# The second layer normalisation moves from ScalarE to VectorE in a gated recurrent layer with a feed-forward part

## The chip, the cores and the metric

One core of one Trainium2 chip runs the kernel. The metric is the device time of one execution, in microseconds. It is compared with the same kernel before the change.

## The reference

The input x has 2 sequences of 4096 steps with 256 features. The layer computes, in float32:

```
u = x @ W_in + b_in;   g = sigmoid(x @ W_gate + b_gate)
h_t = tanh(h_(t-1) @ A + u_t @ Bm)              # 64 states, one step after the other
y_t = g_t * (h_t @ C.T + u_t @ D.T) + (1 - g_t) * x_t
x1  = norm(x + (y @ W_out + b_out + x))
f   = gelu(x1 @ bw1.T + b1) @ bw2.T + b2        # 1024 hidden units, weights are signs times a row scale
out = norm(x1 + f)
norm(v) = (v - mean(v)) / sqrt(var(v) + 1e-5)   # over the 256 features
```

The change touches only how the last line, the second norm, is carried out.

## The kernel before, in words

The 8192 rows are cut into 128 chunks, one for each partition, of 64 steps. Four steps make a block, so a block is 512 rows (four tiles t of 128 rows x 256 features), and there are NB = 16 blocks, numbered n. The first third of the time goes to the recurrence (two sweeps, and the gates). The second part runs all the rest in one software pipeline: `for n in range(-1, NB + 1)` each engine has its own function `iteration(n)`, in which pieces of several blocks stand in an order written out by hand. No planner is at work: the order in each function is the order on that engine's queue, and semaphores tie the queues together.

TensorE's iteration n makes the hidden products `hidden(n, c)` for eight chunks c (L886) and the products back to 256 features `ffn_out(n, c)` (L898), and between them the output product of the recurrence of block n+1 and n+2 (`out_products`, L862), transposes of x1 of block n+1 (L871), and `y_products` (L846) for n+2 and n+3. A hidden product goes through one of three PSUM banks: ScalarE takes the gelu (`hidden_gelu`, L527) and a float16 high part (`hidden_hi`, L535), VectorE makes the float16 low part (`hidden_lo`, L1188). `hidden(n, c)` may overwrite a bank only after the `hidden_lo` that last read it; `hidden(n + 1, 0)` so waits for `hidden_lo(n, 6)`. `ffn_out(n, c)` waits for `hidden_lo(n, c)`.

VectorE's iteration n runs, in this order: hidden_lo(n-1, 6); the second moments of block n-2 (`second_moments`, L1214); hidden_lo(n-1, 7); first sum and spread of block n+1; gate_y(n+2, 1) (L1140); hidden_lo(n, 0); the scale and residual sum of block n-1 (`ffn_scale` L1194, `second_sum` L1201); more of the first norm of block n+1, with hidden_lo(n, 1) to (n, 3) between; first_norm (L1172) and `second_spread(n-1, 0)` (L1206); then hidden_lo(n, 4), x1_lo(n+1, 0) (L1180), hidden_lo(n, 5), x1_lo(n+1, 1), gate_y(n+3, 0), second_spread(n-1, 1), and in iterations 0 to 2 one `keep_x` (L1067). x1_lo waits for ScalarE's x1_hi (L515).

GpSimd's iteration n: mix(n+2, 0) (L361, after gate_y), residual(n) (L377), second_rstd(n-2), mix(n+2, 1), hu_low (L353), ys_low(n+2, 0) (L365), the two first_rstd of block n+1 (L383, L385, after VectorE's first moments), hu_low, ys_low(n+2, 1), add_bias(n+2) (L371).

The second norm of block b: VectorE leaves mean and variance of each row in `moments[:, 1, t]`. GpSimd's second_rstd(b) adds eps (L390), takes minus the mean (L391), raises to the power -1/2 (L394) and multiplies the two (L396): a scale and a shift, kept for each block. ScalarE then applies them in place to `rows_of(gT, b)`, one activation of 128x256 for each tile (`second_norm`, L541): tile 0 in iteration b+2, tiles 1 to 3 in iteration b+3. SP stores the block (L301). For the last block ScalarE does tiles 0 and 1 (L608) and VectorE tiles 2 and 3 (L1316), and SP stores tiles 2 and 3 first (L310), then 0 and 1 (L312).

SP's own loop issues `load_x(n+2)`, which waits for first_sum of block n+1, and then `store(n-3)`.

Of the kernel before, what the change touches and what calls it, by code (L numbers as in the profile page):

```python
# [50 lines left out]
def gated_rnn_ffn(nc, x, W_in, b_in, W_gate, b_gate, A, Bm, C, D, W_out, b_out, w1, b1, w2, b2, out):  # L51
# [7 lines left out]
    NB = L // STEPS  # L59
# [13 lines left out]
    with ExitStack() as ctx:  # L73
        def sb(name, shape, dt=F32):
            return ctx.enter_context(nc.sbuf_tensor(name, shape, dt))

        def sem(name):
            return ctx.enter_context(nc.semaphore(name))
# [32 lines left out]
        neg_one = sb("neg_one", [P, STEPS])  # L111
# [19 lines left out]
        rstd2 = sb("rstd2", [P, NB, STEPS])  # L131
        shift2 = sb("shift2", [P, NB, STEPS])
# [65 lines left out]
        s_e2 = sem("second_norm_steps")  # L198
        s_rs2 = sem("second_scale_and_shift_ready")
# [65 lines left out]
        def due(b, first=0, end=NB):  # L265

            return first <= b < end
# [5 lines left out]
        def _(sp):  # L273
# [29 lines left out]
            for n in range(-1, NB + 2):  # L303
                if due(n + 2, 1):
                    load_x(n + 2)
                if due(n - 3, 0, NB - 1):
                    store(n - 3)
            at = L - STEPS
            sp.wait_ge(s_or_last, 1)
            sp.dma_start(out_rows[:, at + 2:at + 4, :], rows_of(gT, NB - 1)[:, 2:4, :]).then_inc(s_st, 16)  # L310
            sp.wait_ge(s_or, NB)
            sp.dma_start(out_rows[:, at:at + 2, :], rows_of(gT, NB - 1)[:, 0:2, :]).then_inc(s_st, 16)  # L312
# [4 lines left out]
        def _(pool):  # L317
# [4 lines left out]
            pool.memset(neg_one[:, :], -1.0)  # L322
# [64 lines left out]
            def second_rstd(b, tiles, moments_done, steps_done):  # L387

                pool.wait_ge(s_v2, moments_done)
                pool.tensor_tensor(rstd2[:, b, tiles], moments[:, 1, tiles, 1], eps[:, tiles], ALU.add)  # L390
                pool.tensor_tensor(shift2[:, b, tiles], moments[:, 1, tiles, 0], neg_one[:, tiles],  # L391
                                   ALU.mult).then_inc(s_e2, 1)
                pool.wait_ge(s_e2, steps_done + 1)
                pool.tensor_tensor(rstd2[:, b, tiles], rstd2[:, b, tiles], neg_half[:, tiles], ALU.pow).then_inc(s_e2, 1)  # L394
                pool.wait_ge(s_e2, steps_done + 2)
                pool.tensor_tensor(shift2[:, b, tiles], shift2[:, b, tiles], rstd2[:, b, tiles],  # L396
                                   ALU.mult).then_inc(s_rs2, 1)
# [3 lines left out]
            def iteration(n):  # L401
# [4 lines left out]
                if due(n - 2, 0, NB - 1):  # L406
                    second_rstd(n - 2, ALL_TILES, n - 1, n * 2 - 4)
# [37 lines left out]
            second_rstd(NB - 1, slice(0, 2), NB, NB * 2 - 2)  # L445
            second_rstd(NB - 1, slice(2, 4), NB + 1, NB * 2)
# [3 lines left out]
        def _(act):  # L450
# [87 lines left out]
            def second_norm(b, t):  # L538

                act.wait_ge(s_rs2, b + 1)  # L540
                done = nc.scalar.activation(rows_of(gT, b)[:, t, :], rows_of(gT, b)[:, t, :], ACT.Identity,  # L541
                                            bias=shift2[:, b, t:t + 1], scale=rstd2[:, b, t:t + 1])
                if t == STEPS - 1:
                    done.then_inc(s_or, 1)

            def iteration(n):
# [5 lines left out]
                if due(n - 3, 0, NB - 1):  # L552
                    second_norm(n - 3, 1)
# [9 lines left out]
                if due(n - 3, 0, NB - 1):  # L563
                    second_norm(n - 3, 2)
# [8 lines left out]
                if due(n - 3, 0, NB - 1):  # L573
                    second_norm(n - 3, 3)
                if due(n - 2, 0, NB - 1):
                    second_norm(n - 2, 0)
# [29 lines left out]
            act.wait_ge(s_rs2, NB)  # L606
            for t in range(2):
                done = nc.scalar.activation(rows_of(gT, NB - 1)[:, t, :], rows_of(gT, NB - 1)[:, t, :], ACT.Identity,  # L608
                                            bias=shift2[:, NB - 1, t:t + 1], scale=rstd2[:, NB - 1, t:t + 1])
            done.then_inc(s_or, 1)  # L610

# [350 lines left out]
        def _(dve):  # L962
# [246 lines left out]
            def second_moments(n):  # L1209
                dve.wait_ge(s_sp2, n * 2 + 2)  # L1210
                if n > 0:
                    dve.wait_ge(s_rs2, n)
                for t in range(STEPS):
                    done = nc.vector.bn_aggr(moments[:, 1, t, :], stats[:, 1, t, :])  # L1214
                done.then_inc(s_v2, 1)

            def iteration(n):
# [89 lines left out]
            dve.wait_ge(s_rs2, NB - 1)  # L1307
# [5 lines left out]
            dve.wait_ge(s_rs2, NB + 1)  # L1313
            for t in PAIRS[1]:
                row = rows_of(gT, NB - 1)[:, t, :]
                done = nc.vector.tensor_scalar(row, row, rstd2[:, NB - 1, t:t + 1], shift2[:, NB - 1, t:t + 1],  # L1316
                                               ALU.mult, ALU.add)
            done.then_inc(s_or_last, 1)
# [24 lines left out]
```

## Time and profile before

| | us |
|---|---|
| median of 3 runs | 513.57 (511.14 to 516.47) |
| profiled execution, its own time | 514.47 |
| span of its trace | 512.6 |
| busy: PE | 475.2 (93%) |
| busy: VectorE | 374.2 (73%) |
| busy: ScalarE | 302.7 (59%) |
| busy: GpSimd | 278.2 (54%) |

The profile names engines PE (matmul), PEld (weight load), DVE (VectorE), ACT (ScalarE), POOL (GpSimd) and SP (the queue that issues the loads and stores). L886 is line 886 of the kernel before. Times are from the first instruction. A duration reaches from the issue of an instruction to its end; instructions of one engine overlap by some hundredths of a microsecond, so the distance from one start to the next is what each adds to a queue. "[0.39 <-ACT hid L535]" says that the engine sat idle for 0.39 us before this row and what released it. The granted clock is that of TensorE, 1.00 for its full speed.

### The profile page before, as it was taken

To read this page: it belongs to the slowest core of one execution; us is meant where nothing else is said; L and a number is where in the kernel's file an instruction comes from. 1 tells how busy PE (TensorE), PEld (TensorE's weight loads), DVE (VectorE), ACT (ScalarE), POOL (GpSimd) and SP (SyncE) were. 2 spreads that over 40 slices of the span, in tenths; PEclk is the share of its full clock that TensorE was granted. 3 is DMA by queue.
4 is the path that set the end of the run, shared out by engine and by line. 5 is a ranking of instruction groups with operands and counts; after the bars stand their busy time and mean duration, and the time that the engine had idled before them with its cause. 6 is when DMAs were issued, how large, how long until landed. Compare 5 with 4: busy or idle time off the path is not lost.

```text
span 512.6 us, 8565 instructions
## 1 busy us (share of the span) xinstructions
PE 475.2 (93%) x2847; PEld 321.1 (63%) x2847; DVE 374.2 (73%) x784; ACT 302.7 (59%) x550; POOL 278.2 (54%) x289
## 2 busy tenths in 40 slices
PE   9999999999998469989899999999999999999891
PEld 6666566556554247666667766776767767776651
DVE  1455555796976428789898798798797897887664
ACT  1122222443443418748688788797797797787683
POOL 4100010152516748697697787877967976963403
PEclk9999999999999859999999999999999999999997
DMA  7333451000010101101022022021021120220113
GB/s 210 117 107 98 123 196 51 2 0 0 0 43 0 41 1 42 42 1 42 1 83 82 2 83 82 3 83 52 32 83 32 53 83 6 79 83 1 42 41 123
DMA packets 9268, 28.76 MB, mean 56 GB/s; under 512 B 1776, under 2 KB 2544, under 8 KB 9104
## 3 DMA queue, kind: packets, MB, share of 16 engines
q1 hardware_dynamic: 7904, 27.27, 15.7%
q0 software_dynamic: 272, 0.66, 0.4%
q10 hardware_dynamic: 1056, 0.36, 0.3%
q8 instruction: 21, 0.34, 0.3%
q14 instruction: 15, 0.12, 0.1%
HBM read 19.90 MB, written 8.39 MB: 55 GB/s over the span
## 4 chain that ended last, share of the span: by engine, by line
PE 72%; DVE 14%; issue 5%; POOL 5%; ACT 4%; DVEq 0%; POOLq 0%; ACTq 0%
PE bank L886 17%; PE bank L898 16%; PE bank L627 8%; PE bank L724 7%; PE bank L634 7%; DVE hid L1188 5%; PE bank L862 4%; PE bank L846 4%; PE bank L619 4%; DVE gT L1201 3%; ACT hid L535 2%; PE bank L871 2%; DVE bank L1194 2%; DVE bank L1151 2%; PE bank L710 1%
## 5 line engine op out<-in xcount | busy, mean ns | idle before, releaser
L886 PE MATMUL bank<-xT,w1s 128*128 128x512 f16 x512 | 132.3, 382 | 10.0 <-DVE hid L1188 9.7
L898 PE MATMUL bank<-w2s,hid 128*128 128x256 f16 x1024 | 127.6, 273 | 1.3 <-DVE gT L1201 0.8
L1188 DVE SCALAR_TENSOR_TENSOR hid<-bank,small,hid 128x512 f16<-128x512 f32 x128 | 94.1, 737 | 46.8 <-ACT hid L535 46.8
L898 PEld LDWEIGHTS bank<-w2s,hid 128*128 128x128 f16 x1024 | 98.8, 98 | 34.2 <-issue 4.8
L527 ACT ACTIVATE bank<-bank,b_col,alpha 128x512 f32<-128x512 f32 x128 | 95.3, 746 | 36.2 <-PE bank L886 36.0
L535 ACT ACTIVATE hid<-bank,small 128x512 f16<-128x512 f32 x128 | 85.6, 683 | 32.6 <-PE bank L898 31.5
L348 POOL TENSOR_TENSOR xg_lo<-xT,xg_hi 128x512 fp32r<-128x512 f32 x12 | 22.9, 1925 | 104.9 <-DVE xg_hi L991 104.9
L886 PEld LDWEIGHTS bank<-xT,w1s 128*128 128x128 f16 x512 | 45.5, 98 | 54.1 <-issue 12.1
L365 POOL TENSOR_TENSOR ys_lo<-gT,ys_hi 128x512 fp32r<-128x512 f32 x32 | 41.5, 1300 | 45.0 <-ACT ys_hi L511 43.9
L361 POOL TENSOR_TENSOR gT<-gT,xT 128x512 f32<-128x512 f32 x32 | 41.7, 1307 | 16.3 <-DVE gT L1140 14.6
L478 ACT ACTIVATE hu<-bank 64x128 f32 (+1 forms) x64 | 17.4, 272 | 53.6 <-PE bank L634 53.6
L634 PE MATMUL bank<-hu,w_rec 128*64 (+1 forms) x208 | 45.2, 299 | 0.8 <-DVE hu L1013 0.8
L627 PE MATMUL bank<-xT,w_in 128*128 (+1 forms) x128 | 44.9, 435 | 0.0
L371 POOL TENSOR_TENSOR x_load<-x_load,half_b_out 128x1024 f32<-128x1024 f32 x16 | 38.2, 2390 | 10.8 <-DMA x_load<-in_L_attn_x 10.8
L862 PE MATMUL bank<-w_out_hi,ys_hi 128*128 128x256 f32 x128 | 40.7, 318 | 1.4 <-POOL ys_lo L365 1.4
L377 POOL TENSOR_TENSOR gT<-x_rows,b_row 128x1024 f32<-128x1024 f32 x16 | 40.0, 2498 | 2.1 <-DVE x_rows L1172 2.1
L634 PEld LDWEIGHTS bank<-hu,w_rec 128*64 128x64 f32 x208 | 20.0, 135 | 28.7 <-issue 25.7
L466 ACT ACTIVATE hu<-bank 64x128 f32 x40 | 10.9, 271 | 45.7 <-PE bank L634 45.7
L965 DVE COPY xT<-bank 128x256 f32 (+1 forms) x64 | 26.4, 423 | 15.5 <-PE bank L619 14.3
L970 DVE TENSOR_SCALAR hu<-bank,b_in_col 64x256 f32 (+1 forms) x32 | 15.7, 491 | 29.3 <-PE bank L627 29.3
L353 POOL TENSOR_TENSOR hu_lo<-hu,hu_hi 64x512 fp32r<-64x512 f32 x28 | 35.4, 1265 | 2.2
L862 PE MATMUL bank<-w_out_lo,ys_hi 128*128 128x256 f32 x128 | 36.6, 286 | 0.0
(128 smaller groups left out, 843.6 us busy)
## 6 DMA issues: line engine op xcount, KB each, us to landing
x_load<-in_L_attn_x SPq DMA_DIRECT2D x16, 512.0 KB, 3.4
gT<-in_L_attn_x SPq DMA_DIRECT2D x15, 512.0 KB, 3.4
out_rows<-gT SPq DMA_DIRECT2D x15, 512.0 KB, 2.6
gT<-in_L_ffn_w SPq DMA_DIRECT2D x2, 1024.0 KB, 7.2
gT<-in_L_attn_x SPq DMA_DIRECT2D x4, 128.0 KB, 3.0
out_rows<-gT SPq DMA_DIRECT2D x2, 256.0 KB, 2.2
w_gate<-in_L_attn_W_gate ACTq DMA_DIRECT2D x1, 256.0 KB, 7.6
x_rows<-in_L_attn_W_out POOLq DMA_DIRECT2D x1, 256.0 KB, 6.5
```

What stands on the lines that cost most here:

```text
L361: pool.tensor_tensor(gT[:, b, m, :], gT[:, b, m, :], xT[:, b, m, :], ALU.subtract).then_inc(s_ys, 1)
L365: pool.tensor_tensor(ys_lo[:, m, :], gT[:, b, m, :], ys_hi[:, m, :].bitcast(F32), ALU.subtract).then_inc(s_ylo, 1)
L371: pool.tensor_tensor(x_load[:, :, :], x_load[:, :, :], half_b_out[:, None, :].broadcast_to([P, STEPS, DM]), ALU.add).then_inc(s_xb, 1)
L377: pool.tensor_tensor(rows_of(gT, b), x1_rows[:, :, :], b2_row[:, None, :].broadcast_to([P, STEPS, DM]), ALU.add).then_inc(s_x1b, 1)
L527: nc.scalar.activation(bank[which][:, :], bank[which][:, :], ACT.Gelu, bias=b1_col[:, c:c + 1], scale=alpha1[:, c:c + 1]).then_inc(s_gelu, 1)
L535: nc.scalar.activation(hid[:, c % 3, 0, :], bank[HIDDEN_BANKS[c % 3]][:, :], ACT.Copy, scale=hid_scale[:, 0:1]).then_inc(s_hhi, 1)
L627: done = nc.tensor.matmul(bank[4 + half][:, 0:N // 2], w_in[:, k, :], xT[:, j, k, half * (N // 2):(half + 1) * (N // 2)], start=(k == 0), ...
L634: nc.tensor.matmul(bank[6 + parity][0:NS, 0:P], w_rec[:, :], hu[:, t, :], start=True, stop=True).then_inc(done_sem, 1)
L862: done = nc.tensor.matmul(bank[6 + pair][:, e * DM:(e + 1) * DM], ys, w[:, k, :], start=(i == 0), stop=(i == len(parts) - 1))
L886: done = nc.tensor.matmul(bank[which][:, :], w1s[:, k, c * P:(c + 1) * P], x1T[:, n, part, :, k, :], start=(k == 0 and part == 0), stop=(k ...
L898: done = nc.tensor.matmul(bank[tile // 2][:, tile % 2 * DM:(tile % 2 + 1) * DM], hid[:, c % 3, part, tile * P:(tile + 1) * P], w2s[:, c, : ...
L1188: nc.vector.scalar_tensor_tensor(out=hid[:, c % 3, 1, :], in0=bank[HIDDEN_BANKS[c % 3]][:, :], scalar=hid_scale[:, 0:1], in1=hid[:, c % 3, ...
```

## The change

The second norm of every block is carried out by VectorE, in place, as (v - mean) times the inverse root, both read as scalars for each partition. In iteration n it stands in two pairs of tiles: one after hidden_lo(n, 4), one after hidden_lo(n, 5), both for block n-2. GpSimd keeps only the sum with eps and the power; the shift, its constant and the arrays for each block go. ScalarE has no part in it any more. SP stores block n-2 in iteration n, and for the last block tiles 0 and 1 before 2 and 3. In iteration NB, where no hidden chunks are left, the two pairs of block NB-2 stand behind hidden_lo(NB-1, 7) and ahead of the last ffn_scale.

```diff
-        neg_one = sb("neg_one", [P, STEPS])
...
-        rstd2 = sb("rstd2", [P, NB, STEPS])
-        shift2 = sb("shift2", [P, NB, STEPS])
+        rstd2 = sb("rstd2", [P, STEPS])
...
@@ SP
-                if due(n - 3, 0, NB - 1):
-                    store(n - 3)
+                if due(n - 2, 0, NB - 1):
+                    store(n - 2)
             at = L - STEPS
+            sp.wait_ge(s_or, NB)
+            sp.dma_start(out_rows[:, at:at + 2, :], rows_of(gT, NB - 1)[:, 0:2, :]).then_inc(s_st, 16)
             sp.wait_ge(s_or_last, 1)
             sp.dma_start(out_rows[:, at + 2:at + 4, :], rows_of(gT, NB - 1)[:, 2:4, :]).then_inc(s_st, 16)
-            sp.wait_ge(s_or, NB)
-            sp.dma_start(out_rows[:, at:at + 2, :], rows_of(gT, NB - 1)[:, 0:2, :]).then_inc(s_st, 16)
@@ GpSimd
-            pool.memset(neg_one[:, :], -1.0)
...
-            def second_rstd(b, tiles, moments_done, steps_done):
-
-                pool.wait_ge(s_v2, moments_done)
-                pool.tensor_tensor(rstd2[:, b, tiles], moments[:, 1, tiles, 1], eps[:, tiles], ALU.add)
-                pool.tensor_tensor(shift2[:, b, tiles], moments[:, 1, tiles, 0], neg_one[:, tiles],
-                                   ALU.mult).then_inc(s_e2, 1)
-                pool.wait_ge(s_e2, steps_done + 1)
-                pool.tensor_tensor(rstd2[:, b, tiles], rstd2[:, b, tiles], neg_half[:, tiles], ALU.pow).then_inc(s_e2, 1)
-                pool.wait_ge(s_e2, steps_done + 2)
-                pool.tensor_tensor(shift2[:, b, tiles], shift2[:, b, tiles], rstd2[:, b, tiles],
-                                   ALU.mult).then_inc(s_rs2, 1)
+            def second_rstd(b, tiles, done):
+
+                pool.wait_ge(s_v2, done)
+                pool.tensor_tensor(rstd2[:, tiles], moments[:, 1, tiles, 1], eps[:, tiles], ALU.add).then_inc(s_e2, 1)
+                pool.wait_ge(s_e2, done)
+                pool.tensor_tensor(rstd2[:, tiles], rstd2[:, tiles], neg_half[:, tiles], ALU.pow).then_inc(s_rs2, 1)
...
@@ ScalarE (second_norm and its calls in iteration, and the two tiles of the last block)
-            def second_norm(b, t):
-
-                act.wait_ge(s_rs2, b + 1)
-                done = nc.scalar.activation(rows_of(gT, b)[:, t, :], rows_of(gT, b)[:, t, :], ACT.Identity,
-                                            bias=shift2[:, b, t:t + 1], scale=rstd2[:, b, t:t + 1])
...
@@ VectorE
             def second_moments(n):
                 dve.wait_ge(s_sp2, n * 2 + 2)
-                if n > 0:
-                    dve.wait_ge(s_rs2, n)
...
+            def second_norm(b, pair, done):
+
+                dve.wait_ge(s_rs2, done)
+                for t in PAIRS[pair]:
+                    row = rows_of(gT, b)[:, t, :]
+                    last = nc.vector.tensor_scalar(row, row, moments[:, 1, t, 0:1], rstd2[:, t:t + 1],
+                                                   ALU.subtract, ALU.mult)
+                return last
...
                 if due(n):
                     hidden_lo(n, 4)
+                if due(n - 2, 0, NB - 1):
+                    second_norm(n - 2, 0, n - 1)
                 if due(n + 1, 1):
                     x1_lo(n + 1, 0)
                 if due(n):
                     hidden_lo(n, 5)
+                if due(n - 2, 0, NB - 1):
+                    second_norm(n - 2, 1, n - 1).then_inc(s_or, 1)
                 if due(n + 1, 1):
                     x1_lo(n + 1, 1)
...
-            dve.wait_ge(s_rs2, NB - 1)
             for pair in range(2):
                 dve.wait_ge(s_sp2, NB * 2 - 1 + pair)
                 for t in PAIRS[pair]:
                     done = nc.vector.bn_aggr(moments[:, 1, t, :], stats[:, 1, t, :])
                 done.then_inc(s_v2, 1)
-            dve.wait_ge(s_rs2, NB + 1)
-            for t in PAIRS[1]:
-                row = rows_of(gT, NB - 1)[:, t, :]
-                done = nc.vector.tensor_scalar(row, row, rstd2[:, NB - 1, t:t + 1], shift2[:, NB - 1, t:t + 1],
-                                               ALU.mult, ALU.add)
-            done.then_inc(s_or_last, 1)
+            second_norm(NB - 1, 0, NB).then_inc(s_or, 1)
+            second_norm(NB - 1, 1, NB + 1).then_inc(s_or_last, 1)
```

## Rows read from the trace of the kernel before

**Rows 1.** The page: the chain that ended last, its shares of the span by engine.
```profile
PE 72%; DVE 14%; issue 5%; POOL 5%; ACT 4%; DVEq 0%; POOLq 0%; ACTq 0%
```

**Rows 2.** Busy time in one block: stretch, its length, engines, clock, DMA share, GB/s.
```profile
366.08:385.85 19.77, 19.39 (x135) 14.03 (x136) 16.64 (x41) 15.88 (x27) 15.49 (x17) 1.00 0.15 54
```

**Rows 3.** Timeline of VectorE, end of block 8: start us, us, instruction, count.
```profile
360.49 0.74 DVE L1188 SCALAR_TENSOR_TENSOR hid<-bank,small,hid 128x512 f16<-128x512 f32 x1
361.55 0.69 DVE L1180 SCALAR_TENSOR_TENSOR xT<-bank,xT 128x512 f16<-128x512 f32 x1 [0.32 <-ACT xT L515]
362.16 0.74 DVE L1188 SCALAR_TENSOR_TENSOR hid<-bank,small,hid 128x512 f16<-128x512 f32 x1
362.85 0.69 DVE L1180 SCALAR_TENSOR_TENSOR xT<-bank,xT 128x512 f16<-128x512 f32 x1
...
364.06 0.74 DVE L1206 BATCH_NORM_STATS2 stats<-gT 128x6 f32<-128x256 f32 x2
365.18 0.75 DVE L1188 SCALAR_TENSOR_TENSOR hid<-bank,small,hid 128x512 f16<-128x512 f32 x1 [0.39 <-ACT hid L535]
```

**Rows 4.** Timeline of TensorE in block 8: hidden(8, 4) and its wait.
```profile
355.93 1.04 PE L886 MATMUL bank<-xT,w1s 128*128 128x512 f16 x4 [0.36 <-DVE hid L1188]
```

**Rows 5.** Timeline around the end of block 14: hidden_lo(14, 6) and hidden(15, 0).
```profile
482.27 0.75 DVE L1188 SCALAR_TENSOR_TENSOR hid<-bank,small,hid 128x512 f16<-128x512 f32 x1 [0.57 <-ACT hid L535]
...
483.17 1.02 PE L886 MATMUL bank<-xT,w1s 128*128 128x512 f16 x4 [1.75 <-DVE hid L1188]
```

**Rows 6.** Groups by line and shape: busy us, mean ns of one | idle before.
```profile
L541 ACT ACTIVATE gT<-gT,shift,rstd 128x256 f32<-128x256 f32 x60 | 33.9, 595 | 0.9 <-POOL shift L396 0.9
L1172 DVE TENSOR_SCALAR x_rows<-bank,moments,rstd 128x256 f32<-128x256 f32 x64 | 31.3, 531 | 0.2 <-POOL rstd L385 0.2
...
L1316 DVE TENSOR_SCALAR gT<-gT,rstd,shift 128x256 f32<-128x256 f32 x2 | 0.7, 410 | 2.7 <-POOL shift L396 2.7
...
L1081 DVE TENSOR_SCALAR half_b_out<-half_b_out 128x256 f32<-128x256 f32 x1 | 0.3, 284 | 0.0
```

**Rows 7.** Timeline of the end of the kernel, from the last blocks' norms on.
```profile
500.70 1.01 POOL L394 TENSOR_TENSOR rstd<-rstd,neg_half 128x4 f32<-128x4 f32 x1
...
501.96 1.30 DVE L1194 TENSOR_TENSOR bank<-bank,alpha_row 128x512 f32<-128x512 f32 x2 [1.14 <-PE bank L898]
...
508.77 0.73 DVE L1316 TENSOR_SCALAR gT<-gT,rstd,shift 128x256 f32<-128x256 f32 x2 [2.73 <-POOL shift L396]
...
509.91 0.43 SPq L312 DMA_DIRECT2D out_rows<-gT  x1
```

**Rows 8.** Timeline of VectorE and GpSimd in the first part, around 105 us.
```profile
103.43 2.28 DVE L1034 SCALAR_TENSOR_TENSOR gT<-gT 128x2048 f16<-128x2048 f32 x1
103.59 6.53 POOL L348 TENSOR_TENSOR xg_lo<-xT,xg_hi 128x512 fp32r<-128x512 f32 x2 [7.66 <-DVE xg_hi L991]
...
105.63 3.37 DVE L1036 SCALAR_TENSOR_TENSOR gT<-gT 128x2048 f16<-128x2048 f32 x1
```

**Rows 9.** The copies of L1277: count, ns min/median/max, first and last start, forms.
```profile
L1277 DVE COPY hu<-hu x8: 208/219/1194, 151.5 to 158.4; 64x128 f32<-64x128 f32 x8
```

**Rows 10.** Timeline of GpSimd, end of block 8, beside rows 3.
```profile
359.96 1.27 POOL L365 TENSOR_TENSOR ys_lo<-gT,ys_hi 128x512 fp32r<-128x512 f32 x1
361.19 2.37 POOL L371 TENSOR_TENSOR x_load<-x_load,half_b_out 128x1024 f32<-128x1024 f32 x1
```

**Rows 11.** Timeline of GpSimd and VectorE in blocks 13 and 14.
```profile
459.35 0.74 DVE L1188 SCALAR_TENSOR_TENSOR hid<-bank,small,hid 128x512 f16<-128x512 f32 x1
...
461.14 2.37 POOL L377 TENSOR_TENSOR gT<-x_rows,b_row 128x1024 f32<-128x1024 f32 x1
...
478.00 0.74 DVE L1188 SCALAR_TENSOR_TENSOR hid<-bank,small,hid 128x512 f16<-128x512 f32 x1
478.15 2.36 POOL L377 TENSOR_TENSOR gT<-x_rows,b_row 128x1024 f32<-128x1024 f32 x1 [2.13 <-DVE x_rows L1172]
```

**Rows 12.** Busy time and clock in the long idle before the first hidden product.
```profile
176.00:184.00 8.00, 0.32 (x1) 0.35 (x2) 0.00 (x0) 0.96 (x2) 7.27 (x6) 0.50 0.00 0
```

More of the change, by code:

```diff
@@ L197, in gated_rnn_ffn @@
         s_v2 = sem("second_moments_ready")
-        s_e2 = sem("second_norm_steps")
-        s_rs2 = sem("second_scale_and_shift_ready")
+        s_e2 = sem("second_variance_with_eps")
+        s_rs2 = sem("second_rstd_ready")
         s_x1 = sem("x1_ready")
@@ L406, in iteration @@
                 if due(n - 2, 0, NB - 1):
-                    second_rstd(n - 2, ALL_TILES, n - 1, n * 2 - 4)
+                    second_rstd(n - 2, ALL_TILES, n - 1)
                 if due(n + 2, 2):
@@ L444, in _ @@
                 iteration(n)
-            second_rstd(NB - 1, slice(0, 2), NB, NB * 2 - 2)
-            second_rstd(NB - 1, slice(2, 4), NB + 1, NB * 2)
+            second_rstd(NB - 1, slice(0, 2), NB)
+            second_rstd(NB - 1, slice(2, 4), NB + 1)
         @block.scalar
@@ L536, in hidden_hi @@
                                      scale=hid_scale[:, 0:1]).then_inc(s_hhi, 1)
-            def second_norm(b, t):
-                act.wait_ge(s_rs2, b + 1)
-                done = nc.scalar.activation(rows_of(gT, b)[:, t, :], rows_of(gT, b)[:, t, :], ACT.Identity,
-                                            bias=shift2[:, b, t:t + 1], scale=rstd2[:, b, t:t + 1])
-                if t == STEPS - 1:
-                    done.then_inc(s_or, 1)
             def iteration(n):
@@ L551, in iteration @@
                     hidden_hi(n - 1, 7)
-                if due(n - 3, 0, NB - 1):
-                    second_norm(n - 3, 1)
                 if due(n):
@@ L562, in iteration @@
                     hidden_gelu(n, 2)
-                if due(n - 3, 0, NB - 1):
-                    second_norm(n - 3, 2)
                 if due(n + 3, 2):
@@ L572, in iteration @@
                     hidden_hi(n, 3)
[L573 to L576, printed above, removed]
                 if due(n):
@@ L605, in _ @@
                 iteration(n)
[L606 to L610, printed above, removed]
         @block.tensor
```

## The prediction, made before the change was timed

> **What bounds the kernel now.** Read the page first: the chain that ended last runs on PE for 72% and on DVE for 14% [rows 1], so TensorE carries the time and VectorE cuts in. Then one block of the second half, from hidden(n, 0) to hidden(n+1, 0). I number blocks by n; block 9 is 366.08 to 385.85, and the ten blocks 3 to 12 repeat it every 19.77 us. In that time ACT is busy 15.88, POOL 15.49, DVE 16.64, PE 19.39 [rows 2]. The averages do not say what ends a block; the queues do. hidden(n+1, 0) needs hidden_lo(n, 6) from VectorE. In block 8 that instruction starts at 365.18 [rows 3], and the matmul that opens block 9 at 366.08, 0.90 later. Block 14 shows that 0.90 is the hand-over itself: hidden_lo at 482.27, matmul at 483.17, and there PE had waited 1.75 us for it [rows 5]. So in blocks 3 to 12 PE and VectorE arrive together, and VectorE has no slack towards TensorE.
>
> What slack VectorE has inside its stream is in two places, both inside the stretch where the change inserts work [rows 3]. After hidden_lo(4) at 360.49 the next instruction could start 0.69 later (as 362.16 to 362.85), at 361.18, but x1_lo waits to 361.55: 0.37. The last pair of statistics starts at 364.06; its two take 0.74 and the next could start some 0.67 later, at 364.73, but hidden_lo(6) waits for ScalarE to 365.18: 0.45. Together 0.82 us a block.
>
> **The change part by part.** *ScalarE* loses 60 activations of 595 ns in the blocks [rows 6], 2.4 us each block, and two at the end. I cost this at nothing gained. Both waits of VectorE for ScalarE above are for work that TensorE had released just before (x1_hi follows the transposes, hidden_hi(6) follows hidden_gelu(7)), and no second_norm stands between; the other PE wait, 0.36 before hidden(n, 4) [rows 4], is for hidden_lo(1), which stands in VectorE's own queue behind the scale and sum instructions. ys_high comes earlier by 0.6, but GpSimd's next result for VectorE follows VectorE's own moments.
>
> *GpSimd* loses the multiply by -1 and the shift product, about 0.3 us of queue with the dependent wait, in a stretch after which it idles for ys_high. Nothing. The constant memset at the start is hidden under the input loads.
>
> *SP* stores a block one iteration earlier. The store waits for the second pair's norm and stands ahead of the next load_x, which waits for a first_sum half a block later. Nothing queues.
>
> *VectorE* gains four tensor_scalar of 128x256 a block. The form is there: two at the end, 410 ns each, 0.73 for the two [rows 6, 7], so they start 0.32 apart and a pair adds 0.66 to the stream. Four add 1.32. Against 0.82 of slack that alone is 0.50 a block.
>
> *The collision.* I do not stop there. The same operation reading PSUM takes 531, from SBUF 410, which is 121 less; one with constants in SBUF takes 284 [rows 6]. 128 of 256 columns at one a cycle would be about that difference: the SBUF form seems to take two elements at a time. The Trainium skill ("VectorE: DVE Perf Modes", the perf-mode tier table) says that fp32 tensor_scalar within SBUF runs at 2x, using both read ports; the 410 beside 531 agrees. By its cycle estimate one norm would be about 290 ns, by the row it is 410; the sum takes the row.
>
> This matters since instructions of VectorE that read SBUF twice at a time and GpSimd's shut each other out in this trace [rows 8]. VectorE's L1034 runs 2.28 us from 103.43; GpSimd's two L348, from 103.59, take 6.53 together, where one of 512 elements takes 1.27 [rows 10]. VectorE's next, L1036, is issued at 105.63 and takes 3.37 against its twin's 2.28, 1.09 more: it let the L348 that was waiting pass first, nearly whole. They alternate, each waiting for one full instruction of the other. L1034 has two sources in SBUF; that one source is enough is seen in the eight small SBUF copies of L1277, 219 ns in the median and 1194 at most [rows 9], the long ones beside GpSimd's work. The Trainium skill ("SBUF — State Buffer", SBUF: two separate sides) calls it an exclusive lock held for the full instruction; these rows agree.
>
> Now place the first pair. It is issued at 361.18. GpSimd ends ys_low(1) at 361.23 and starts add_bias (L371, 2.37 us) at 361.19 [rows 10]. Both engines are tied to VectorE's moments there, so this meeting recurs in each block. The first norm gets in, ends at about 361.56, add_bias follows from about 361.43 to 363.80, and the second norm, issued at 361.50, comes behind it and ends 0.29 later, at 364.09. (If add_bias wins the first turn both norms come after it, with the same end.) The pair takes 2.91 instead of 0.73, so 2.18 more. The second pair falls after add_bias; GpSimd's next instruction, mix, waits for a gate_y that stands behind it on VectorE, so it is free.
>
> Blocks 3 to 12: 1.32 + 2.18 - 0.82 = 2.68, times 10 = 26.8. Block 2 also carries keep_x and has no second slack: 3.50 - 0.37 = 3.1. Block 13: GpSimd has add_bias and residual back to back, the second from 461.14 for 2.37 [rows 11]; hidden_lo(4) starts at 459.35 [rows 11], so the pair is issued at 460.04; its first norm passes between the two, the second after residual, and it ends near 463.98, 3.94 instead of 0.73. That is 3.21 + 1.32, less the slack of this block, 0.37 + 0.65 (the idle before hidden_lo(6) is 0.57, as in block 14 [rows 5]): 3.5. Block 14: hidden_lo(4) at 478.00, residual 478.15 to 480.51 [rows 11]; the pair, issued at 478.69, ends at 481.12, 2.43 instead of 0.73: 1.70 + 1.32 - 1.02 = 2.0. Block 15: VectorE idles more than a pair before each place: 0. Sum 35.4.
>
> *The end.* norm(14) now stands on VectorE ahead of the last ffn_scale (501.96). It waits for the pow that starts at 500.70 [rows 7], 0.15 earlier without the multiply, so it runs from 501.6 to 502.9: +0.95. At the very end four small GpSimd instructions go from the path (0.87 with their waits), of which I give back 0.4 since norm and the second pow meet: -0.5. The store that SP issues last is no longer second in line (it began at 509.91, and the norm before it ended at 509.50): -0.38. Together +0.1.
>
> **Sum.** 35.5 us on the profiled execution's 514.47 gives 550.0. That execution lies 0.9 above the median of 513.57, so I forecast 549.
>
> The unknown cost is the wait of a norm behind GpSimd. Below it is nothing (0.50 a block); the longest blocking of VectorE that I show is 1.09 (3.37 - 2.28), by a 512-element instruction; above it is 2.37 a turn, full length of add_bias. I take 2.18, since rows 8 show full length each time and L371 is the instruction that stands there. With +-0.3 us on each block the forecast's own range is 544 to 554.
>
> **Rivals.**
> *No collision* (the two pointer scalars keep the norm to one port, or both norms slip in before add_bias). For it: 410 ns is also what one element a cycle could give, and the second norm misses its turn by only 0.3 us. Against: 121 ns less than from PSUM, and both queues keep step with the same moments. Time: 0.50 x 10 + 1.0 + 0.3 x 2 - 0.3 = +6.3, 520. Chance 0.10.
> *Short lock* (a GpSimd instruction of 1024 elements lets go half way, 1.09): 1.59 x 10 + 2 + 3 + 0 = +21, 534. Chance 0.07.
> *Not slower*: its place is the 0.82 us of slack a block. If norms follow each other by 0.20 instead of 0.32, as their place behind a wait might hide, and no lock bites, four fit into it; this decides at 0.205 a norm. Blocks 3 to 15 then cost 0, block 2 0.4, the end -0.3: 514. ScalarE's free 2.4 us speaks for it, the measured 0.32 against. Chance 0.03.
> *Slower still*: the longer wait of PE, 2.7 us in one piece, makes the clock fall. After the long idle of 176 to 184 it was granted 0.50 (1.2 of 2.4 GHz) [rows 12]; the wait of 1.75 in block 14 left the four matmuls behind it at 1.02 us, as in a block at full clock [rows 4, 5]. PE's part of the loop, hidden(0) to ffn_out(6), is five groups of eight or four matmuls, some 0.9 each (the four of hidden(0) show 1.02); these 4.4 us would double: 4.4 x 12 = 53 more, 602. Chance 0.03.
> The forecast has 0.77.
>
> **Numbers.** Less than 1% of 513.57, about 5 us, can't be told from no change. Slower by more: 0.77 + 0.07 + 0.03 and half of no collision, 0.92. Within: the other half and most of not slower, 0.06. Faster 0.02. The range takes in the forecast with its bounds (to 558, if both norms of a pair wait a turn in some blocks) and goes down to 527, which leaves out no collision and takes in the short lock: 0.77 x 0.95 + 0.07 = 0.80.
>
> **What would show it.** In the profile after: blocks of about 22.4 us; a pair of norms of 2.9 us on VectorE that begins right after hidden_lo(4), beside L371; the second pair 0.73; x1_lo(0) without a wait; PE waiting some 2.7 us before hidden(n+1, 0), released by hidden_lo(6); ScalarE down by 36 us. If both pairs are 0.73 and blocks last 20.3, the collision was wrong and the stream argument right; if blocks last 19.8, both were. A granted clock under 1.00 between 250 and 450 would be the last rival.

## The result: 9% slower, and the profile after

The changed kernel took 565.12 us in the median (557.43 to 567.45 in 4 runs) against 512.42 for the kernel before. The ratio is 1.0915, with a 95% interval of 1.0853 to 1.0977; it is below the quotient of the medians because it leaves out the two runs that took over 1.5% longer than the quickest. The profiled execution shown below is the one of 565.87 us. Its granted clock is 0.949, as in the run of 564.38 us; the quickest run, 557.43 us, has 0.960. The forecast was 549, with 558 as the upper end.

Its page, first the span, then busy time by engine, the slices of the granted clock, and the chain that ended last [rows 1]:

```profile
span 563.9 us, 8515 instructions
...
PE 497.8 (88%) x2847; PEld 330.1 (59%) x2847; DVE 419.6 (74%) x846; ACT 274.3 (49%) x488; POOL 275.3 (49%) x254
...
PEclk9999999999998799989898998989989898899997
...
PE 47%; DVE 40%; issue 5%; POOL 4%; ACT 2%; DVEq 0%; POOLq 0%; ACTq 0%
```

VectorE's share of the chain went from 14% to 40%: TensorE now waits for it in every block. ScalarE's busy time fell from 302.7 to 274.3 us, and the kernel was slower all the same (what that relief is worth by itself is experiment 8). And the clock slices are dented in the second half, where [rows 2] had 1.00 throughout a block.

The group of the new instruction, and how its single durations spread (count, ns min/median/max):

```profile
L1190 DVE TENSOR_SCALAR gT<-gT,moments,rstd 128x256 f32<-128x256 f32 x64 | 50.1, 824 | 2.0 <-POOL rstd L389 2.0
```

```profile
L1190 DVE TENSOR_SCALAR gT<-gT,moments,rstd x64: 397/403/2470, 241.6 to 561.1; 128x256 f32<-128x256 f32 x64
```

A mean of 824 over a median of 403 says that a few instances are very long. The timeline of VectorE at the end of block 8 shows which (it answers to [rows 3]; L1158 is hidden_lo, L1150 x1_lo, L1190 the norm):

```profile
385.54 0.74 DVE L1158 SCALAR_TENSOR_TENSOR hid<-bank,small,hid 128x512 f16<-128x512 f32 x1
386.19 2.78 DVE L1190 TENSOR_SCALAR gT<-gT,moments,rstd 128x256 f32<-128x256 f32 x2
388.89 0.68 DVE L1150 SCALAR_TENSOR_TENSOR xT<-bank,xT 128x512 f16<-128x512 f32 x1
389.50 0.73 DVE L1158 SCALAR_TENSOR_TENSOR hid<-bank,small,hid 128x512 f16<-128x512 f32 x1
390.15 0.72 DVE L1190 TENSOR_SCALAR gT<-gT,moments,rstd 128x256 f32<-128x256 f32 x2
...
392.66 0.73 DVE L1158 SCALAR_TENSOR_TENSOR hid<-bank,small,hid 128x512 f16<-128x512 f32 x1
```

and GpSimd at the same time (L362 is ys_low, L368 add_bias; compare [rows 10]):

```profile
385.00 1.27 POOL L362 TENSOR_TENSOR ys_lo<-gT,ys_hi 128x512 fp32r<-128x512 f32 x1
386.23 2.59 POOL L368 TENSOR_TENSOR x_load<-x_load,half_b_out 128x1024 f32<-128x1024 f32 x1
```

The first pair of norms takes 2.78 us and spans the whole of add_bias, which itself takes 2.59 instead of 2.37, since it starts beside the first norm. The second pair, with GpSimd idle, takes 0.72. Neither x1_lo nor hidden_lo(6), at 392.66, waits for ScalarE any more.

What TensorE does with that, at the start of block 9 (L856 is a hidden product, L816 y_products, L868 ffn_out), against [rows 4, 5]:

```profile
393.53 1.46 PE L856 MATMUL bank<-xT,w1s 128*128 128x512 f16 x4 [2.15 <-DVE hid L1158]
394.43 0.99 PE L816 MATMUL bank<-hu_hi,cd_hi 128*128 128x512 f32 x1
395.22 0.63 PE L816 MATMUL bank<-hu_hi,cd_lo 128*128 128x512 f32 x1
395.64 0.63 PE L816 MATMUL bank<-hu_lo,cd_hi 128*128 128x512 f32 x1
396.07 1.69 PE L868 MATMUL bank<-w2s,hid 128*128 128x256 f16 x8
397.60 1.03 PE L856 MATMUL bank<-xT,w1s 128*128 128x512 f16 x4
```

and by stretch, PE to POOL busy, then the granted clock; the first line is all of block 8 (block 9 in [rows 2] is its like), the next three follow the clock at the start of block 9, and the last two are the first 7 us of blocks 13 and 14:

```profile
369.72:393.53 23.81, 21.24 (x134) 14.79 (x135) 19.84 (x45) 14.08 (x22) 15.40 (x15) 0.93 0.13 45
393.00:394.00 1.00, 0.47 (x3) 0.26 (x4) 1.00 (x6) 0.00 (x0) 1.00 (x2) 0.99 0.02 4
394.00:397.00 3.00, 3.00 (x11) 1.76 (x10) 2.36 (x5) 1.38 (x2) 2.90 (x3) 0.50 0.00 0
397.00:398.00 1.00, 1.00 (x7) 0.65 (x6) 0.00 (x1) 0.00 (x0) 0.92 (x1) 0.81 0.00 0
...
489.04:496.04 7.00, 7.00 (x37) 4.63 (x38) 3.04 (x9) 1.68 (x3) 4.65 (x4) 0.76 0.01 2
512.91:519.91 7.00, 7.00 (x50) 5.21 (x51) 4.69 (x12) 3.96 (x6) 1.22 (x2) 1.00 0.02 6
```

TensorE waits 2.15 us for hidden_lo(6), begins at full clock, and is granted 0.50 (1.2 of 2.4 GHz) from about 394 to past 397, some 3.4 us. The eight ffn_out matmuls take 1.69 instead of the 1.05 that the same eight took in block 9 before. The four hidden matmuls from 397.60 take 1.03, as at full clock. The first 7 us of a block show 0.76 or 0.77 in all eleven blocks 3 to 13, and 1.00 in blocks 2 and 14.

**Where the 51.3 us are** (spans 563.9 and 512.6). Blocks 3 to 12 last 238.3 us together instead of 197.7, 4.06 more each. In block 9 this splits at 399.60, the start of hidden_hi(9, 0) on ScalarE: up to there it is 6.07 us from the block's start, before 4.44 (+1.63, all of it lost at the low clock); from hidden_lo(9, 0) to hidden_lo(9, 6) it is 16.14, before 13.71 (+2.43). The same stretch takes 6.07 or 6.08 in the other blocks up to 13, apart from 5.99 in block 3 and 6.34 in block 11 (which has 0.3 more in experiment 6 too, at full clock). With eleven blocks at the low clock: 11 x 1.63 = 17.9. The stream costs 10 x 2.43 = 24.3 in blocks 3 to 12, 2.86 in block 2 (no fall there), 4.52 - 1.63 = 2.9 in block 13 and 1.77 in block 14 (PE's wait ahead of it was 1.56, and no fall): 31.8. Block 15 with the end is +1.1 and what lies ahead of block 2 is +0.4. Sum 51.2. The +1.1 hides a twelfth fall of the clock: from hidden(15, 0) to hidden_hi(15, 0) it is 5.41 instead of 3.73, so 1.7 lost, against which the end itself is shorter (experiment 10).

### The profile page after: what moved, and what is told of

It is laid out like the page before. It is cut to its first block, busy times and chain, and to the rows that moved or that the text cites. A ratio compares the mean times of both kernels' runs of the same rounds, so it can differ in the third digit from the quotient of the medians.

```text
span 563.9 us, 8515 instructions
## 1 busy us (share of the span) xinstructions
PE 497.8 (88%) x2847; PEld 330.1 (59%) x2847; DVE 419.6 (74%) x846; ACT 274.3 (49%) x488; POOL 275.3 (49%) x254
## 4 chain that ended last, share of the span: by engine, by line
PE 47%; DVE 40%; issue 5%; POOL 4%; ACT 2%; DVEq 0%; POOLq 0%; ACTq 0%
DVE hid L1158 10%; PE bank L856 8%; DVE gT L1190 8%; PE bank L868 7%; PE bank L597 7%; PE bank L694 7%; PE bank L604 6%; DVE x_rows L1142 4%; DVE stats L1176 3%; PE bank L589 3%; PE bank L816 3%; DVE xT L1150 3%; DVE gT L1171 2%; ACT hid L527 2%; DVE bank L1164 2%
## 5 line engine op out<-in xcount | busy, mean ns | idle before, releaser
L856 PE MATMUL bank<-xT,w1s 128*128 128x512 f16 x512 | 138.6, 396 | 37.3 <-DVE hid L1158 37.2
L868 PE MATMUL bank<-w2s,hid 128*128 128x256 f16 x1024 | 134.1, 281 | 1.3 <-DVE gT L1171 0.8
L1158 DVE SCALAR_TENSOR_TENSOR hid<-bank,small,hid 128x512 f16<-128x512 f32 x128 | 93.9, 735 | 51.3 <-ACT hid L527 51.3
L868 PEld LDWEIGHTS bank<-w2s,hid 128*128 128x128 f16 x1024 | 102.2, 102 | 40.1 <-issue 8.5
L856 PEld LDWEIGHTS bank<-xT,w1s 128*128 128x128 f16 x512 | 46.2, 99 | 82.9 <-issue 41.3
L362 POOL TENSOR_TENSOR ys_lo<-gT,ys_hi 128x512 fp32r<-128x512 f32 x32 | 41.6, 1302 | 54.7 <-ACT ys_hi L503 53.7
L1190 DVE TENSOR_SCALAR gT<-gT,moments,rstd 128x256 f32<-128x256 f32 x64 | 50.1, 824 | 2.0 <-POOL rstd L389 2.0
L368 POOL TENSOR_TENSOR x_load<-x_load,half_b_out 128x1024 f32<-128x1024 f32 x16 | 40.7, 2543 | 10.8 <-DMA x_load<-in_L_attn_x 10.8
L350 POOL TENSOR_TENSOR hu_lo<-hu,hu_hi 64x512 fp32r<-64x512 f32 x28 | 35.5, 1267 | 2.2
```

The lines of the kernel that those rows point to most:

```text
L362: pool.tensor_tensor(ys_lo[:, m, :], gT[:, b, m, :], ys_hi[:, m, :].bitcast(F32), ALU.subtract).then_inc(s_ylo, 1)
L368: pool.tensor_tensor(x_load[:, :, :], x_load[:, :, :], half_b_out[:, None, :].broadcast_to([P, STEPS, DM]), ALU.add).then_inc(s_xb, 1)
L856: done = nc.tensor.matmul(bank[which][:, :], w1s[:, k, c * P:(c + 1) * P], x1T[:, n, part, :, k, :], start=(k == 0 and part == 0), stop=(k ...
L868: done = nc.tensor.matmul(bank[tile // 2][:, tile % 2 * DM:(tile % 2 + 1) * DM], hid[:, c % 3, part, tile * P:(tile + 1) * P], w2s[:, c, : ...
L1158: nc.vector.scalar_tensor_tensor(out=hid[:, c % 3, 1, :], in0=bank[HIDDEN_BANKS[c % 3]][:, :], scalar=hid_scale[:, 0:1], in1=hid[:, c % 3, ...
L1190: last = nc.vector.tensor_scalar(row, row, moments[:, 1, t, 0:1], rstd2[:, t:t + 1], ALU.subtract, ALU.mult)
```

## The experiments

Two theories stood after the result. The first: the growth of a block is a collision of the first pair with add_bias (about 2.05), plus the norms' own time beyond the slack (0.35), plus a clock loss that the longer wait of TensorE sets off (1.63). The second: the norms, their pointer scalars or their position cost this by themselves, and the clock merely goes with it. Each experiment takes one piece away. All are edits of the changed kernel, unless said otherwise. A block is the distance between hidden(n, 0) and hidden(n+1, 0) in blocks 3 to 12; it was 19.77 before and 23.81 after.

**1. add_bias cut to four columns** (the bias is then missing from most of x_load; the instruction stays in its place).

```diff
-pool.tensor_tensor(x_load[:, :, :], x_load[:, :, :], half_b_out[...].broadcast_to([P, STEPS, DM]), ALU.add)
+pool.tensor_tensor(x_load[:, 0, 0:4], x_load[:, 0, 0:4], half_b_out[:, 0:4], ALU.add)
```

> The changed kernel with GpSimd's add_bias cut from 1024 to 4 columns (most of half the output bias is left out of the sum; nothing else changes). Theory 1, the second norm of a pair waits behind add_bias: the first pair falls from 2.78 us to about 0.73, TensorE's wait before hidden(n+1, 0) from 2.15 to about 0.5, the granted clock stays at 1.00, a block lasts about 20.3 instead of 23.8, in all about 519 us. Theory 2, the norms are slow in the stream for a reason of their own (in place, two pointer scalars): the pair stays at 2.78 and the time near 557 to 565.

Measured: 521.41 us, ratio to the kernel before 1.0136 (1.0115 to 1.0156). VectorE and GpSimd at the meeting point, then TensorE behind it (the norm is L1189 here):

```profile
381.28 0.72 DVE L1189 TENSOR_SCALAR gT<-gT,moments,rstd 128x256 f32<-128x256 f32 x2
...
381.31 0.42 POOL L368 TENSOR_TENSOR x_load<-x_load,half_b_out 128x4 f32<-128x4 f32 x1
...
386.56 1.02 PE L855 MATMUL bank<-xT,w1s 128*128 128x512 f16 x4 [0.38 <-DVE hid L1157]
```

The pair is 0.72, TensorE waits 0.38 instead of 2.15, the block is 20.12 and the four matmuls take 1.02. One instruction on another engine, shortened, gives back 3.7 of 4.06 us a block. What is left, 0.35, is the four norms less the slack. Block 15, which follows a wait of 3.51 here, still began at a low clock (0.62 over its first 7 us).

**2. add_bias cut to 512 columns** (half of the bias is missing).

```diff
-pool.tensor_tensor(x_load[:, :, :], x_load[:, :, :], half_b_out[...].broadcast_to([P, STEPS, DM]), ALU.add)
+pool.tensor_tensor(x_load[:, 0:2, :], x_load[:, 0:2, :], half_b_out[...].broadcast_to([P, 2, DM]), ALU.add)
```

> The changed kernel with add_bias cut from 1024 to 512 columns (half of half the output bias is left out). Theory 1, a norm waits for the whole of add_bias: that instruction falls from 2.37 to about 1.3 us and the first pair from 2.78 to about 1.7; block 21.1, TensorE waits about 1.35 us and its clock holds; in all about 533 us. A lock held for a fixed time or let go half way: the pair at 2.0 or over.

Measured: 535.32 us, ratio 1.0393 (1.0324 to 1.0462). The same three places:

```profile
390.59 1.70 DVE L1190 TENSOR_SCALAR gT<-gT,moments,rstd 128x256 f32<-128x256 f32 x2
...
390.63 1.50 POOL L368 TENSOR_TENSOR x_load<-x_load,half_b_out 128x512 f32<-128x512 f32 x1
...
396.84 1.02 PE L856 MATMUL bank<-xT,w1s 128*128 128x512 f16 x4 [1.34 <-DVE hid L1158]
```

The pair's extra is 0.98 behind 512 columns and 2.06 behind 1024, so it follows the full length of GpSimd's instruction; the rival "short lock", by which the 1024 columns let go after 1.09, is out. The block is 21.09, and with a wait of 1.34 the clock held in blocks 4 to 13. It fell in block 3, behind 3.12, and in block 15, behind 3.52.

**3. A control: the kernel before, with add_bias cut to four columns in it.**

> Control: the kernel before with add_bias cut to 4 columns, as in the run of the changed kernel. Theory 1: add_bias is on no path of the kernel before, so 0 to 1 us less than before, and the gain of the cut in the changed kernel was the collision alone. Rival: shorter GpSimd work itself saves 10 us or more, here as there.

Measured: 511.66 us, ratio 0.9942 (0.9916 to 0.9968), blocks of 19.77 as before. Shortening add_bias gives about 3 us by itself, more than I expected, and none of it in blocks 1 to 15: block 0 begins at 185.81 instead of 187.66 and lasts 1.0 less, the latter by the clock, which was 0.85 over its first 7 us in the trace of the kernel before and 1.00 here. So the block times of experiments 1 and 2 are due to the meeting with the norms, but of the total of experiment 1 some 3 us are not. For the 512 columns of experiment 2 no such control was run.

**4. The norm's access pattern changed, everything else left** (252 instead of 256 columns of each tile, read as three runs of 84 that lie 85 apart, written as one run; the values written are then not all the right ones).

```diff
-nc.vector.tensor_scalar(row, row, moments[:, 1, t, 0:1], rstd2[:, t:t + 1], ...)
+nc.vector.tensor_scalar(row[:, 0:252].rearrange("p (a c) -> p a c", a=3),
+                        row[:, 0:255].rearrange("p (a c) -> p a c", a=3)[:, :, 0:84],
+                        moments[:, 1, t, 0:1], rstd2[:, t:t + 1], ...)
```

> The changed kernel with each second norm reading 3 rows of 84 columns (a pitch of 85) and writing 252 in one row, instead of 256 to 256: four columns are left out and the others shifted, the work is the same size, but the shape should keep VectorE from taking two elements at a time. Theory 1, a norm meets GpSimd only because it reads SBUF twice at a time: each norm alone takes longer (about 0.53 instead of 0.41), none waits for add_bias, the first pair takes about 1.0 instead of 2.78, a block lasts 20.6, in all about 526 us. Theory 2, any norm in SBUF waits for GpSimd: the pair stays at 2.8 or more, 557 to 565.

Measured: 526.64 us, ratio 1.0248 (1.0185 to 1.0311). The spread of the norm's durations, then the meeting:

```profile
L1190 DVE TENSOR_SCALAR gT<-gT,moments,rstd x64: 522/534/543, 241.7 to 521.5; 128x252 f32<-128x252 f32 x64
```

```profile
387.73 0.98 DVE L1190 TENSOR_SCALAR gT<-gT,moments,rstd 128x252 f32<-128x252 f32 x2
...
387.78 2.37 POOL L368 TENSOR_TENSOR x_load<-x_load,half_b_out 128x1024 f32<-128x1024 f32 x1
```

This is the cleanest answer. The norm is slower (534 for 252 columns against 403 for 256), yet the longest of 64 is 543 instead of 2470, add_bias takes its undisturbed 2.37, and the kernel takes 38 us less than the changed one in the median, 31 less than its quickest run. So the access pattern decides: as written, the norm is 131 ns quicker and is shut out; with the other pattern it is neither. That the quicker form takes two elements at a time fits the 131 ns, but the trace doesn't show it by itself. The Trainium skill ("VectorE: DVE Perf Modes", What auto-detection actually checks) lets an operation with one source run on two ports where source and destination are in SBUF and their outermost dimensions are both even or equal; three runs into one are neither, and the 534 agrees.

**5. Both pairs moved behind x1_lo(n+1, 1)**, the first by three VectorE instructions, the second by one, nothing left out.

```diff
-if due(n - 2, 0, NB - 1): second_norm(n - 2, 0, n - 1)
 ...
-if due(n - 2, 0, NB - 1): second_norm(n - 2, 1, n - 1).then_inc(s_or, 1)
 ...
+if due(n - 2, 0, NB - 1): second_norm(n - 2, 0, n - 1)
+if due(n - 2, 0, NB - 1): second_norm(n - 2, 1, n - 1).then_inc(s_or, 1)
```

> The changed kernel with both norm pairs moved two and one places later on VectorE, behind x1_lo(n+1, 1) and ahead of gate_y(n+3, 0), where add_bias is about to end and GpSimd's next instruction waits for that gate_y. Same instructions, same count. Theory 1, the meeting with add_bias costs: no norm takes much over its 0.41, four add 1.3 to 1.5 us against 0.45 of slack, a block lasts 20.7 to 20.8, the wait of TensorE is about 1 us and the clock holds; in all about 525 us. Theory 2, four more instructions on VectorE cost what they cost wherever they stand: 557 to 565.

Measured: 527.35 us, ratio 1.0244 (1.0218 to 1.0269).

```profile
389.24 0.69 DVE L1150 SCALAR_TENSOR_TENSOR xT<-bank,xT 128x512 f16<-128x512 f32 x1 [0.32 <-ACT xT L507]
...
391.15 1.38 DVE L1190 TENSOR_SCALAR gT<-gT,moments,rstd 128x256 f32<-128x256 f32 x4
...
394.58 1.02 PE L856 MATMUL bank<-xT,w1s 128*128 128x512 f16 x4 [0.84 <-DVE hid L1158]
```

The same work at another place in the same queue: the four norms take 1.38 together and the block 20.58. They cost 0.81 instead of the 0.35 of experiment 1, since the idle time before x1_lo(0), 0.32, is back and unused. The change as made cost 53 us in the median (45 in its quickest run), the same four norms a little further on cost 13: the rest was the place.

**6. The clock held up by other matmuls.** Nine matmuls of 512 columns into a bank that is free, right before hidden(n+1, 0); their result is overwritten.

```diff
+if due(n, 2, NB - 2):
+    pe.wait_ge(s_hlo, n * HC + 6)
+    for i in range(9):
+        nc.tensor.matmul(bank[HIDDEN_BANKS[2]][:, :], w1s[:, 0, 0:P], x1T[:, n, 0, :, 0, :], start=True, stop=True)
```

> The changed kernel with nine more matmuls of 512 columns on TensorE in blocks 2 to 13, into a free bank, between the output products and hidden(n+1, 0), so that TensorE works while it waits for VectorE. Theory 1, the wait of 2.15 us makes the clock fall to half for the 3 to 4 us behind it, and that costs 1.6 us a block: the clock stays at 1.00, hidden(n, 0) to hidden_hi(n, 0) takes 4.4 us again instead of 6.1, a block 22.2, in all about 545 us. Theory 2, TensorE's clock costs nothing since VectorE sets the pace: no change, or some us slower from the added matmuls.

Measured: 546.83 us, ratio 1.0630 (1.0608 to 1.0652). VectorE's pair (L1195 here), then TensorE with the added matmuls (L916), then five blocks of it by clock:

```profile
376.40 2.78 DVE L1195 TENSOR_SCALAR gT<-gT,moments,rstd 128x256 f32<-128x256 f32 x2
...
381.43 2.12 PE L916 MATMUL bank<-xT,w1s 128*128 128x512 f16 x9
383.74 1.02 PE L856 MATMUL bank<-xT,w1s 128*128 128x512 f16 x4 [0.19 <-DVE hid L1163]
```

```profile
282.80:394.00 111.20, 108.23 (x718) 74.17 (x716) 99.02 (x212) 70.40 (x111) 77.08 (x72) 1.00 0.15 49
```

The collision is untouched (2.78), TensorE does more work, and the kernel takes 18 us less than the changed one in the median, 11 less than its quickest run. Blocks last 22.18, which is 1.63 less than 23.81, and from hidden(n, 0) to hidden_hi(n, 0) it is 4.44 again instead of 6.07: this shows that the 1.63 was the clock's. It also comes near the forecast's sum with its clock assumption made true: +32 us on the 514.71 that the kernel before took beside it, where I had +35.5. Block 15 still began at a low clock, behind a wait of 3.53.

**7. Four such matmuls instead of nine.**

> As the run with nine added matmuls, but with four, so that TensorE still waits about 1.25 us before hidden(n+1, 0) instead of 0.2. If the clock is lost to the length of the wait, 1.25 us is as harmless as the 1.34 and 1.75 us seen before: clock 1.00, block 22.2, 547 us. If any wait in this place cools the clock, blocks of 23 to 24 us, 557 or more.

Measured: 548.73 us, ratio 1.0680 (1.0611 to 1.0749); blocks of 22.18 again.

```profile
382.54 1.04 PE L916 MATMUL bank<-xT,w1s 128*128 128x512 f16 x4
384.84 1.02 PE L856 MATMUL bank<-xT,w1s 128*128 128x512 f16 x4 [1.27 <-DVE hid L1163]
```

About 1 us of work, which cuts the wait to 1.27, is enough in blocks 4 to 13, all at 1.00. In block 3 the wait was still 3.04, and in block 15 it was 3.52; behind both the clock fell.

**8. The norm of blocks 0 to 14 left out on VectorE** (their output is then not normalised a second time); ScalarE and GpSimd are relieved as in the change.

> The changed kernel without the second norm of blocks 0 to 14 on VectorE (left out of the output; the store waits for the statistics instead), ScalarE and GpSimd as in the changed kernel. Theory 1, ScalarE's and GpSimd's relief is worth nothing and the whole loss comes from the norms on VectorE: blocks of 19.77 us, the end about 1.2 us shorter, 511 us. Rival, the relief of ScalarE is worth something that the norms hide: 505 us or less.

Measured: 512.97 us, ratio 0.9965 (0.9942 to 0.9988), blocks of 19.77. What is left of the change, the relief of ScalarE and GpSimd and the new end, is worth 1.8 us in all and nothing in the blocks up to 14; in the trace block 15 with the end is 28.00 instead of 29.45, which experiment 10 shows too. So no placement of the norms could have been much faster than the kernel before.

**9. A placement meant to be free**: tiles 0 and 1 behind gate_y(n+2, 1), half a block earlier, tile 2 alone behind hidden_lo(4), tile 3 alone behind x1_lo(1).

```diff
+second_norm(n - 2, (0, 1), n - 1)          # behind gate_y, before hidden_lo(n, 0)
 ...
+second_norm(n - 2, (2,), n - 1)            # behind hidden_lo(n, 4)
 ...
+second_norm(n - 2, (3,), n - 1).then_inc(s_or, 1)   # behind x1_lo(n + 1, 1)
```

> The changed kernel with the norms where VectorE idles and GpSimd does not stand in the way: tiles 0 and 1 behind gate_y(n+2, 1), where VectorE waits 2.4 us for hidden_hi(n, 0); tile 2 behind hidden_lo(n, 4) alone, so that it passes just ahead of add_bias (in blocks 14 and later with tile 3); tile 3 behind x1_lo(n+1, 1). The moments of block 14 move to the end of iteration 15, so that its norms run before the last scale. Theory 1: blocks 3 to 12 back at 19.77, block 2 and 13 some tenths longer, the end 1 us shorter than before: 512 us, level with the kernel before or 0.2% faster. If the place was not the matter, 520 or more.

Measured: 522.02 us, ratio 1.0156 (1.0133 to 1.0179); blocks of 20.65. This missed. VectorE, then GpSimd, around the early pair, and at last tile 2 with add_bias beside it:

```profile
355.70 2.70 DVE L1190 TENSOR_SCALAR gT<-gT,moments,rstd 128x256 f32<-128x256 f32 x2 [0.67 <-POOL rstd L389]
358.32 0.74 DVE L1158 SCALAR_TENSOR_TENSOR hid<-bank,small,hid 128x512 f16<-128x512 f32 x1
...
354.65 1.02 POOL L389 TENSOR_TENSOR rstd<-rstd,neg_half 128x4 f32<-128x4 f32 x1
355.64 1.26 POOL L358 TENSOR_TENSOR gT<-gT,xT 128x512 f32<-128x512 f32 x1
356.98 1.26 POOL L350 TENSOR_TENSOR hu_lo<-hu,hu_hi 64x512 fp32r<-64x512 f32 x1
...
367.99 0.41 DVE L1190 TENSOR_SCALAR gT<-gT,moments,rstd 128x256 f32<-128x256 f32 x1
...
368.01 2.61 POOL L368 TENSOR_TENSOR x_load<-x_load,half_b_out 128x1024 f32<-128x1024 f32 x1
```

The pair waits for GpSimd's root (L389), and the moment it is released is the moment GpSimd starts mix: each norm then sits out one GpSimd instruction, mix and hu_low, and takes 1.35 and 1.42, together 2.70. The two single norms did what was planned: tile 2 slips in ahead of add_bias in 0.41, tile 3 takes 0.47, and from hidden_lo(4) to hidden_lo(6) it is 4.70 us, before 4.69 [rows 3]. So the 0.88 by which a block grew is the early pair's, and a single norm at that place would most likely have waited too, as the first of the pair did.

**10. The kernel before with the new end alone** (block 15's four norms on VectorE, its two stores as in the change).

> The kernel before with only the end of the change: the last block's four tiles by VectorE with mean and root as scalars, no shift on GpSimd for it, tiles 0 and 1 stored first. The collision has no part in it. 0.9 us off GpSimd's chain and 0.3 off the last store: 1.2 us less than before, 0.2%; rival, the last store's own time hides it: no change.

Measured: 513.17 us, ratio 0.999 (0.9964 to 1.0015): no difference that can be told in the times. In its trace block 15 with the end is 28.03 instead of 29.45.

## Why the forecast was right, and where it failed

**What bounds the kernel: right.** The step "PE and VectorE arrive together" held. Where the clock held, TensorE's wait at hidden(n+1, 0) was the growth of the block to 0.03 us: 0.38 and 0.35 (1), 1.34 and 1.32 (2), 0.84 and 0.81 (5).

**ScalarE, GpSimd and SP at nothing: right,** shown by experiment 8 (0.3% in all, most of it at the end). ScalarE's busy time went down by 28 us, not 36.

**Four norms at 0.66 a pair against 0.82 of slack: nearly.** Forecast 0.50 a block, shown 0.35 by experiment 1. The difference lies in hundredths: in its trace, between hidden_lo(4) at 380.62 and hidden_lo(6) at 385.68, a norm follows hidden_lo after 0.66 where 0.69 was counted, twice, and a pair adds 0.64 or 0.65 instead of 0.66.

**The collision: right in mechanism and size.** Forecast: the pair takes 2.91, so 2.18 more. Measured: 2.78, so 2.06 more. The inference from [rows 6, 8, 9] that the norm waits for a full instruction of GpSimd, and only in its quicker form, holds: cutting that instruction to four columns (1), halving it (2), moving away from it (5) and changing the norm's own access (4) each take the wait away, in whole or in the proportion expected. Blocks 13 and 14, with residual as the partner, showed pairs of 3.44 and 2.33 (forecast 3.94 and 2.43). The whole stream part came to 31.8 where I had 35.4.

**The clock: here it failed.** The step was "the wait of 1.75 in block 14 left the four matmuls behind it at 1.02 us", from which I gave the fall of the clock 0.03. I had forecast a wait of 2.7, well beyond the longest that a row showed as harmless [rows 5]; beyond it stood only the 0.50 after a long idle [rows 12]. Between the two the trace said nothing, and I took the harmless end. The runs put in its place: behind 2.15 us (3.92 the first time), in each of eleven blocks, the clock fell to half for about 3.4 us and cost 1.63. The sign that the prediction named for this rival came too: the granted clock was 0.93 between 250 and 465, where before it was 1.00 between 250 and 450. I also built that rival as all or nothing, doubling 4.4 us of PE's part to reach 602. In truth the clock came back within the block: only what was issued in those 3.4 us was slower. That is 17.9 us in the sum that the forecast hadn't, and 1.7 more in block 15, while the rival priced the same mechanism at 53.

**The end: small, but not as forecast.** Forecast +0.1; block 15 with the end is +1.1. The wait before hidden(15, 0) grew to 3.52, and the clock fell behind it too, which cost 1.7:

```profile
533.33 1.32 PE L856 MATMUL bank<-xT,w1s 128*128 128x512 f16 x4 [3.52 <-DVE hid L1158]
534.44 1.92 PE L868 MATMUL bank<-w2s,hid 128*128 128x256 f16 x8
```

Experiment 10 shows that the new end by itself costs nothing; in its trace it saves 1.4. What norm(14) ahead of the last scale costs, 0.95 in the forecast, was not measured alone.

**The sum again.** 31.8 (stream) + 17.9 (clock) + 1.5 (start and end) = 51.2, against 35.5. With the clock kept up in the blocks by four or nine matmuls the kernel takes 549 or 547, close to the forecast's 549. That closeness is in part luck: the stream came out 3.6 us below the forecast, and block 15 lost 1.7 at the low clock that the forecast hadn't.

**Left open.** The quickest of the changed kernel's runs, 557.43 us, had a clock of 0.960 against 0.949 at 565.87. That would fit a clock that fell in fewer blocks. As an estimate, 0.051 of 563.9 us less 0.040 of 555.5 us (the spans) is 6.5 us of full clock, and a fall takes half of 3.4, so about four falls fewer; at 1.63 each they make 6.5 of the 8.4 us. No trace of that run exists.

## What to carry to other kernels

Before VectorE gets an operation between SBUF tensors, look at what GpSimd runs at that very moment: a single such instruction can slip in just ahead of GpSimd's, and a second one right behind it waits out GpSimd's whole instruction. Where GpSimd's own result releases them, GpSimd is already on its next instruction, and even the first one waits. Price the wait that this hands to TensorE twice, once as time and once as clock: where the forecast wait is longer than any that the trace shows as harmless, put a partial clock loss per occurrence into the sum instead of leaving it to a rival. If such a wait can't be avoided, about 1 us of matmuls in it whose result is thrown away can cost less than the clock does.

## What the runs showed of the hardware beyond what was expected

The clock's answer to a wait isn't settled by its length alone. No fall was seen in the blocks behind waits of 0.83, 1.27, 1.34, 1.56 and 1.75 us; there was one behind 2.15 in each block of the changed kernel, and behind 3.52 in block 15. Behind 3.04 (experiment 7) and 3.12 (experiment 2), ahead of block 3, it fell as well. Between 1.9 and 2.7 the outcome varied: ahead of block 3, a wait of 2.62 in experiment 5 was followed by a fall, one of 2.64 in experiment 4, one of 2.17 in experiment 1 and one of 1.97 in experiment 6 by none; ahead of block 15, waits of 2.37 in experiment 5 and 2.40 in experiment 4 were followed by none. By stretch, the first 7 us of block 3 in experiment 5, then in experiment 4:

```profile
248.85:255.85 7.00, 7.00 (x37) 4.38 (x38) 2.92 (x9) 2.29 (x4) 5.09 (x5) 0.76 0.00 0
```

```profile
249.27:256.27 7.00, 7.00 (x49) 5.19 (x50) 4.57 (x11) 3.85 (x6) 5.11 (x5) 1.00 0.01 2
```

What decides between two such waits stays open. The eleven falls of the changed kernel are no eleven trials either: its blocks repeat one timing, and the half-clock stretch moves through it slowly, from 0.15 us before the block's first matmul in block 3 to 0.51 us behind it in block 13. They show that a wait of 2.15 can cost the clock each time, not that it must.

The first matmuls behind a wait may still run at full clock: at 393:394 the grant was 0.99, and 0.50 only from 394 on, and in experiment 5 the four matmuls from 248.85 took their usual 1.02 although the 7 us were granted 0.76. So the four matmuls right behind a wait, which is where I had looked in [rows 5], can look sound while those after them are not; for the wait of 1.75 itself the clock did hold, since the first 7 us of block 15 before (483.17 to 490.17) were granted 1.00.

A norm of 256 columns takes 403 ns in the median as written, and one of 252 columns takes 534 with the other access pattern. Where GpSimd is busy, the slower form makes the faster kernel, 526.64 against 565.12 us.
